# Placing a batch's picks straight behind its routing in the router pipeline of a two-layer transformer kernel

## The reference

```python
logits = jax.nn.relu(x @ rw1 + rb1) @ rw2 + rb2
vals, ids = jax.lax.top_k(logits, K)                      # K = 2 of E = 8
probs = jax.nn.softmax(vals, axis=-1)
m = jax.nn.one_hot(ids_f, E, dtype=jnp.int32)
pos = jnp.cumsum(m, axis=0) - 1                           # slot = picks so far of the same expert
keep = (pos_tok < CAP).astype(x.dtype)                    # CAP = 512
disp = jnp.zeros((E, CAP, Cx), x.dtype).at[ids_f, pos_c].add(xr * keep[:, None])
```

## Time and profile before

| | |
|---|---|
| median of three runs | 1009.13 us (1007.19 to 1015.8) |
| the profiled execution | 1008.39 us, its span 1006.6 us |
| PE busy | 798.5 us (79%) |
| VectorE busy | 678.7 us (67%) |
| ScalarE busy | 621.2 us (62%) |
| GpSimd busy | 630.4 us (63%) |
| mean granted TensorE clock | 0.919 |

### The profile page before, as it was taken

One profiled execution on the slowest core, in us unless ns is written; L12 is line 12 of the kernel. 1 busy time (PEld: TensorE's weight loads), 2 busy tenths in 40 slices (PEclk: granted clock), 3 DMA queues, 4 the chain that ended last, 5 costly groups with the idle time before them and its releaser, 6 DMA issues.

```text
span 1006.6 us, 17882 instructions
## 1 busy us (share of the span) xinstructions
PE 798.5 (79%) x5918; PEld 479.8 (48%) x5918; DVE 678.7 (67%) x1994; ACT 621.2 (62%) x923; POOL 630.4 (63%) x414
## 2 busy tenths in 40 slices
PE   1976465579777629828767688999999999999997
PEld 0443122125323125613222255777777777777776
DVE  5669899965554357749499776866665656666564
ACT  1755133314332327616967837989898888889895
POOL 4008799610545553646588895777777777777685
PEclk9977899978978858969999987999999999999999
DMA  5899200017000020043150000000000000000000
GB/s 132 99 121 204 91 0 0 17 31 204 31 12 7 4 72 25 23 125 96 45 175 1 0 1 1 2 11 0 10 0 10 0 11 0 10 0 10 0 12 12
DMA packets 52694, 40.42 MB, mean 40 GB/s; under 512 B 5995, under 2 KB 44638, under 8 KB 52638
## 3 DMA queue, kind: packets, MB, share of 16 engines
q1 hardware_dynamic: 49566, 37.27, 17.4%
q0 software_dynamic: 3072, 2.51, 0.9%
HBM read 18.05 MB, written 14.88 MB: 33 GB/s over the span
## 4 chain that ended last, share of the span: by engine, by line
PE 55%; DVE 11%; issue 4%; ACT 3%; another core or an unknown queue 3%; DMA 1%; POOL 1%; DVEq 0%; SPq 0%; POOLq 0%; ACTq 0%
PE PS L1684 53%; DVE scratch L1476 3%; DVE scratch L1484 2%; DVE resid L1413 2%; PE PS L1691 2%; ACT scratch L808 1%; DVE stats L1253 1%; POOL disp L600 1%; DVE scratch L1433 0%; DMA A<-disp 0%; PE PS L2080 0%; DVE scratch L1496 0%; DMA A<-y_rows 0%; DMA disp<-A,scratch 0%
## 5 line engine op out<-in xcount | busy, mean ns | idle before, releaser
L686 POOL TENSOR_TENSOR scratch<-scratch 128x1024 f16<-128x1024 f32 x128 | 272.8, 2133 | 105.2 <-ACT scratch L1065 102.3
L1637 DVE SCALAR_TENSOR_TENSOR resid<-PS,coef,resid 128x128 f32<-128x128 f32 x512 | 144.1, 344 | 135.8 <-PE PS L1684 134.0
L1684 PE MATMUL PS<-A,scratch 128*128 128x128 f16 x3456 | 217.4, 219 | 7.4 <-DVE A L1380 5.2
L1684 PEld LDWEIGHTS PS<-A,scratch 128*128 128x128 f16 x3456 | 204.0, 98 | 40.1 <-DVE A L1380 6.5
L1684 PE MATMUL PS<-A 128*128 (+1 forms) x768 | 188.2, 382 | 0.0
L1061 ACT ACTIVATE scratch<-PS,cols 128x512 f32<-128x512 f32 x256 | 164.0, 684 | 15.6 <-PE PS L1684 14.9
L1065 ACT ACTIVATE scratch<-scratch 128x1024 f16<-128x1024 f32 x128 | 135.3, 1057 | 5.2
L1684 PE MATMUL PS<-scratch,ident 128*128 128x512 f32 x160 | 89.5, 683 | 57.8 <-DVE scratch L1220 56.1
L563 POOL TENSOR_TENSOR scratch<-A 128x1024 f32<-128x1024 f32 x32 | 76.0, 2386 | 84.8 <-DVE A L1194 65.6
L600 POOL DMA_INDIRECT disp<-A,scratch x64 | 65.2, 1018 | 70.1 <-DVE scratch L1316 53.1
L1684 PEld LDWEIGHTS PS<-A 128*128 128x128 f16 x768 | 72.4, 99 | 72.0 <-issue 10.4
(11 more groups left out here) (295 smaller groups left out, 1345.9 us busy)
## 6 DMA issues: line engine op xcount, KB each, us to landing
A<-A SPq DMA_DIRECT2D x22, 256.0 KB, 8.4
y_rows<-zeros SPq DMA_DIRECT2D x8, 512.0 KB, 6.0
A<-y_rows SPq DMA_DIRECT2D x16, 256.0 KB, 3.6
disp<-zeros SPq DMA_DIRECT2D x4, 528.0 KB, 21.7
A<-disp SPq DMA_DIRECT2D x4, 528.0 KB, 5.9
resid<-in_L_attn_x SPq DMA_DIRECT2D x8, 256.0 KB, 4.5
A<-scratch SPq DMA_DIRECT2D x8, 256.0 KB, 7.9
A<-in_L_ffn_ew SPq DMA_DIRECT2D x1, 2048.0 KB, 12.9
```

Of the source, the lines that this page charges most:

```text
L686: pool.tensor_tensor(h_low[n % 4], h_full[n % 2], h_high[n % 4], SUB).then_inc(S("m1_low"), 1)
L1637: last = STT(out=resid[:, g, :], in0=bank(4 + e % 2)[:, t * C:(t + 1) * C], scalar=coef[:, t, e:e + 1], in1=resid[:, g, :], op0=MUL, op1=ADD)
L1684: return nc.tensor.matmul(o, l, r, start=start, stop=stop)
```

## The change

In the loop over batches, VectorE's `place_picks(b)` moves from the head of iteration b+1 to the place straight behind `route(b)`, in front of `add_o(b + 2)`. The last call, which stood behind the loop, is now inside it. No instruction is added or removed, no wait and no signal changes; the other engines' lists are the same.

```diff
             for b in range(B):
-                if b:
-                    place_picks(b - 1, 1 - b % 2)
                 if b + 1 < B:
                     normalise5(b + 1)
                 if b + 2 < B:
                     gate_o(b + 2)
                 if b + 1 < B:
                     xT5_low(b + 1)
                 route(b, b % 2)
+                place_picks(b, b % 2)
                 if b + 2 < B:
                     add_o(b + 2)
-            place_picks(B - 1, 1)
```

## The result

The changed kernel takes 1007.85 us (median of 20 runs, 999.29 to 1011.52) beside 1013.43 us for the kernel before (20 runs, 1007.19 to 1020.37). The ratio is 0.9933, with a 95% interval of 0.9909 to 0.9957: 6.8 us faster, between 4.4 and 9.2 (the two medians differ by 5.6). The profiled execution took 1005.03 us with a span of 1003.3, against 1008.39 and 1006.6. The forecast was a gain of 7.5 us, within 1%; both hold. The time itself says little, since the 20 runs of the kernel before lie 4 us above the three that were known: 1007.85 lies in the stated range of 997 to 1009, but above the 997.6 to 1005.3 of the forecast's own theory, and is also the figure of rival 1. The trace decides between them.

A forecast was written before the change was run, and what follows sets the result against it. A loop of waits through several engines, released 1.49 us after each GpSimd burst, was taken as the stage's bound; first burst -2.1, four cycles -6.9, tail +1.5 gave -7.5 us: 1000.9 from 1008.39, theory 997.6 to 1005.3, stated range 997 to 1009.

The forecast's parts named there:

- rival 1: Batches' loop: `lgT5_mm` logits held to the release, mean cycle 16.1 us, no gain in four cycles, 1007.8 us; chance 0.10.
- rival 3: Batches' loop: the burst isn't what releases, TensorE really works that long; 1008.4 to 1010.8 us; chance 0.12.
- The loop and its release: Bursts 1 to 5: late TensorE signals wait until 1.49 us after burst end; 16.1 us loop, floor 13.74 after the change.
- the forecast's own sign: Changed profile: if burst end to release is no longer 1.49 us, rival 3 holds and the loop's reading is wrong.
- First burst: Burst 0: its placing no longer waits behind the addition, so it starts 2.15 us earlier, 251.8 for 253.93.
- Four cycles: Bursts 1 to 5: cycles of 14.4 us, 57.6 for 64.47, a gain of 6.9 us (bounds 9.5 and 4.1).
- the upper bound: Four cycles: logits held to the release, cycles alternating between 16.4 and 13.74 us, 15.1 in the mean; gain 4.1 us.
- the last part: Signs in the changed profile: a wait moved to L1288 means the cycles' upper bound, to L814 rival 1 or 2.
- Tail of the stage: Bursts 5 to 7: batch 7's first hidden parts may be held; loss of 1.5 us (bounds 0.8 and 3.1).
- What follows hangs on burst 7 and shifts with it: Behind burst 7: last DMAs landing, reading back and experts shift with it, some 7.5 us earlier.
- Cost nothing: Addition, statistics and norm moved behind the placing: no loss, or 6 x 0.4 = 2.4 us if their cover were gone.
- Rival 1 and 2: `lgT5_mm` held: in alternate cycles (1: 1007.8 us, chance 0.10) or every cycle (2: 1016.9 us, chance 0.06).

The follow-up runs named there:

- experiment 3: Kernel before with every burst waiting for the slots of batch 5, on a chip where signals are held: 1036.26 us beside 1013.23 us.
- experiment 4: Kernel before with four DMAs per burst: 972.12 us; kernel after with a 2.9 us mid-burst GpSimd pause: 999.52 us, ratio 0.9822 to the kernel before.
- experiments 4 and 5: Mid-burst GpSimd pause of eight clearings, in the kernel after (999.52 us, ratio 0.9822) and in the kernel before (998.28 us, ratio 0.9868).
- the pause kernels: Eight GpSimd clearings between each burst's 4th and 5th DMA, added to the kernel after (999.52 us) and to the kernel before (998.28 us).
- experiment 2: Both kernels unchanged on the chip without held signals: before 972.0 us, after 973.95 (ratio 1.0002); also bias copy moved, 972.78, and late bursts, 1020.38.

## Why the prediction was right, and where its steps were off

**The loop and its release: right, but the rule for what is held was too simple.** The burst is what the loop waits for (experiment 3), and four DMAs hold nothing to their end (experiment 4). That signals wait, and not that TensorE works longer beside a burst, the rows already showed: TensorE starts the counts at 293.08, just behind VectorE's picks, so it is past the hidden parts that stand before them in its list, while ScalarE goes on with these parts only at 295.30. The release was taken as 1.49 us behind the last DMA's end. Now it comes at two distances: 1.5 to 1.8 us (263.29, 292.27), or 0.1 to 0.2 us (275.77 behind 275.65; 359.48 behind 359.28). By the forecast's own sign another distance than 1.49 meant rival 3; that sign was too strict, as experiment 3 shows.

The forecast took its rule (late by 1.6 us at 5.4 us into a burst, held from 6.5 us on) from the cycle of burst 2. In the same trace it doesn't hold for every burst. TensorE and VectorE of the kernel before, in burst 6 (345.21 to 355.11):

```profile
353.51 0.32 PE L1684 MATMUL PS<-scratch,ones 128*128 128x24 f16 x7
```
```profile
353.87 0.19 DVE L1306 TENSOR_TENSOR scratch<-PS,scratch 128x32 f32<-128x32 f32 x1 [0.45 <-issue]
```

These counts are given 8.6 us into the burst and are used at once; in the kernel after the same signal passes 7.9 us into burst 6 (346.98). The other way round, the counts of batch 1 are given only 5.6 us into burst 0 (recorded end 259.49) and reach VectorE at 265.39, 1.3 us behind its end. What tells these cases apart no run shows. For the logits, on which the four cycles hung, the rule served: given 7.3 and 8.1 us into bursts 1 and 3 of the kernel after they are held to the end, given 5.5 and 6.3 us into bursts 2 and 4 they come 2.2 to 2.4 us late inside them.

The Trainium skill's "SBUF — State Buffer", "Who interferes with whom", says that TensorE and ScalarE never wait on anyone. Nothing here contradicts it for ports; as a rule for waits it would have missed 5.8 us in each cycle (16.1 less 10.27).

**First burst, 2.15 us forecast: 2.26 measured.** Right. Burst 1 was to keep this whole, 13.84 us behind burst 0; it is 14.08 behind, so 0.24 us of it is lost. (Before burst 1 of the kernel before GpSimd was idle 3.69 us, and not some 6 as before the next four; nothing hung on that.)

**Four cycles, 57.6 us forecast: 59.39 measured.** The mechanism was right, to the alternation and the place of the new wait (L1288) that the last part named for it; the size lay near the upper bound (60.3), not in the middle. That the middle was taken had no row behind it. A distance is 9.90 us of burst, the gap from its end to L1306, and 2.4 us until the next burst. The four gaps are 2.61 (275.65 to 278.26), 1.81, 4.08 and 1.76 us, for a floor of 1.49. Two are the held logits; the other two are counts that come 0.3 us behind the forecast release. The term is a gain of 5.1 us for 6.9.

**Tail of the stage, 1.5 us of loss forecast: 0.1 measured.** From burst 5 to burst 7 it is 24.24 us for 24.14. Burst 6 is 13.86 us behind burst 5, as forecast (13.74); batch 7's chain isn't later, and burst 7 follows after 0.48 us of idle time. The 1.5 us came from the rule above: the first two hidden parts of batch 7, which "may be held", pass 7.0 to 7.7 us into burst 5 (ScalarE's L808 at 332.32). This error offsets most of that of the cycles, which is luck: burst 7 moved by 7.0 us for 7.5.

**"What follows hangs on burst 7 and shifts with it": this step failed.** Two things change behind burst 7. VectorE's splits no longer run beside the burst, so its last three DMAs take 0.97 us each, where they took 1.71, 1.97 and 1.96 before; the last DMA starts 8.7 us earlier (358.31 for 367.04), and its row ends 9.7 us earlier (359.28 for 369.00). By the distance of before (369.00 to 374.27) the experts could start at 364.55. But the signal for the bias copy, 3.1 us into burst 7 both times, now falls into an unbroken run of two bursts and is held to its end, and the splits behind it end at 367.97, so that the experts start at 369.09, 4.5 us later than they could. Of 9.7 us, 5.2 are left. That it is the two bursts without a gap (0.48 us between them, where the kernel before has 1.27) that hold the signal is argued, not tested: the counts' signal passed 7.9 us into the first of the two. That the late copy costs the 4.5 us, experiments 4 and 5 confirm: same last DMA, copy not held, experts' start at 364.4. I hadn't asked what VectorE does behind its last placing.

**The end.** The 5.2 us are 4.9 at the first scan (499.75 for 504.65) but 3.3 at the span's end. Between the first scan and the table load at the head of the next expert stage (L1061; 611.76 in the kernel before) the kernel before took 107.1 us, the kernel after 108.5 (to 608.29), the pause kernels 108.8 and 108.3, and the kernel before in experiment 2 108.7; so the first is the short one, by 1.4 us that are no work of the change. The ratio over 20 runs each gives 6.8 us (4.4 to 9.2), which covers 4.9. So the forecast of 7.5 came nearer to the measured 6.8 than the traces can account for: they show 5.2 us at the experts' start, and the 1.9 us from 4.9 to 6.8 have no place in them. Part of the agreement may be luck.

**"Cost nothing" for the addition behind the placing: right in itself, but its cover was worth something.** The addition no longer stands over the counts' way to VectorE. In the gaps above, 0.45 us of waiting for the counts is already contained (278.26, 308.72). On the chip without the hold it is all that the change does to a cycle, 0.45 us each, and uses up the first burst's gain.

**The rivals.** Rival 1 and 2 (`lgT5_mm` held) would have shown distances of 18.4 us and a wait at L814; neither is there (16.37 us is the longest, and ScalarE's L814 has no remote wait). Rival 3 fell in experiment 3. What none of them foresaw is that the hold depends on the chip: there the answer is "no change" for another reason.

**Left open.** What holds the signals isn't shown, nor which of them are held, nor why one chip holds none. Whether GpSimd's issuing or the transfers themselves do it, no run separates. That chip was met in two sets of runs; the kernel before lies 36.3 us lower there in its span, of which 32.4 is gained by the experts' start (341.82 for 374.27). Not tried: the bias copy moved where signals are held, where it would start the splits earlier and lengthen burst 7's DMAs instead.

## What to carry to other kernels

When two engines that wait for different signals of a third come free at the same moment, look for what ended just before, on whatever engine; here an unbroken run of indirect DMAs. Moving work out of such a loop gave about half of its length back (5.1 of 9.4 us), because the next signal in line is held in its place; here a pause that moved the run's end into mid-burst gave more, where GpSimd had the time. A rule read from one cycle should be laid against every cycle of the same trace before a sum is built on it. And follow a gain past the stage's last transfer to the next engine that was level with it: 4.5 us were lost to a copy that no one had waited for.

## What the runs showed of the hardware

- On all chips met but one, signals of TensorE given late in a run of eight indirect DMAs (9.9 us) often reached VectorE and ScalarE only 0.1 to 1.8 us behind the run's end, up to 7.0 us after the matmuls' recorded end (359.48 for 352.50). In bursts 1 to 4, logits given 5.4 to 6.4 us in came 1.1 to 2.4 us late inside the run. There were exceptions both ways (counts given 8.6 us into burst 6 of the kernel before passed, counts given 5.6 us into its burst 0 were held). Runs of four DMAs (4.8 us) held nothing to their end.
- This isn't so on every chip: the same program has cycles of 16.1 us and takes 1008 to 1015 us on some, and has cycles of 10.27 us and takes 969 to 973 us on one.
- An indirect DMA of 128 rows takes GpSimd 0.97 us, and 1.97 us beside VectorE's splits (two inputs and an output in SBUF). The Trainium skill's "SBUF — State Buffer", "Who interferes with whom", says that a VectorE instruction with two SBUF inputs contends with GpSimd instructions that read SBUF; these rows agree, if an indirect DMA counts as one that reads SBUF (its rows and slots lie there). ScalarE's splits alone (350.14 to 355.93 in the kernel after) left burst 7's DMAs at 0.97 us.
